# A two-layer graph and expert network on one core: the vector engine's expert chain is interleaved with scores and statistics in the first pass

## What is computed

```
x = x + _L0_gnn_ref(_layernorm(x), adj, W, a)     # attention over neighbours, elu
x = x + _L0_ffn_ref(_layernorm(x), ...)           # 8 experts, top 2 of each row, gelu
x = x + _L1_gnn_ref(_layernorm(x), adj, W, a)     # attention over neighbours, relu
x = x + _L1_ffn_ref(_layernorm(x), ...)           # 32 experts, the best one of each row, relu
```

## Time and profile before

| | us |
|---|---|
| median of three runs | 1150.54 (1149.45 to 1150.75) |
| the profiled execution, its own time | 1146.29 |
| its span from first to last instruction | 1144.6 |

### The profile page before, as it was taken

One profiled execution on the slowest core, in us unless ns is written; L12 is line 12 of the kernel. 1 busy time (PEld: TensorE's weight loads), 2 busy tenths in 40 slices (PEclk: granted clock), 3 DMA queues, 4 the chain that ended last, 5 costly groups with the idle time before them and its releaser, 6 DMA issues. The chain is left out here.

```text
span 1144.6 us, 27026 instructions
## 1 busy us (share of the span) xinstructions
PE 918.4 (80%) x6709; PEld 815.7 (71%) x6709; DVE 790.8 (69%) x3511; ACT 699.9 (61%) x2364; POOL 774.0 (68%) x1039
## 2 busy tenths in 40 slices
PE   5988889887379999999996599999984377656683
PEld 4777778776279999999996488888873255435463
DVE  6689999998569999999996168888887122221122
ACT  3999999896055555555554599999981143323320
POOL 4447887777728777877878017777887366666665
PEclk9999999988589999999999799999995565775655
DMA  9234432213257777878772212233312343232200
GB/s 210 64 98 146 145 102 74 62 53 112 83 162 209 204 205 206 204 201 210 200 202 74 66 38 76 76 80 87 80 40 74 82 121 94 80 87 84 66 21 37
DMA packets 144906, 129.22 MB, mean 113 GB/s; under 512 B 26522, under 2 KB 116511, under 8 KB 144755
## 3 DMA queue, kind: packets, MB, share of 16 engines
q1 hardware_dynamic: 124114, 91.94, 31.9%
q0 software_dynamic: 17760, 34.20, 8.5%
q10 hardware_dynamic: 2880, 1.35, 0.4%
HBM read 82.74 MB, written 47.48 MB: 114 GB/s over the span
## 5 line engine op out<-in xcount | busy, mean ns | idle before, releaser
L546 POOL DMA_INDIRECT xs<-staged,dst x256 | 260.7, 1018 | 76.9 <-issue 68.3
L1258 ACT ACTIVATE hT<-bank,wt 128x128 f32<-128x128 f32 x620 | 177.1, 369 | 123.1 <-PE bank L1488 86.4
L619 POOL DMA_INDIRECT out<-oq,xq x144 | 145.0, 1007 | 96.4 <-DVE oq L1157 57.4
L597 POOL DMA_INDIRECT x2d<-ob,xi x155 | 164.0, 1058 | 42.8 <-issue 28.5
L1470 PE MATMUL bank<-xnT,wt 128*128 128x128 f32 x1240 | 167.5, 279 | 11.1 <-ACT hT L1258 10.0
L1488 PE MATMUL bank<-w2s,hT 128*128 x1240 | 166.3, 277 | 0.6 <-ACT hT L1258 0.5
L1470 PEld LDWEIGHTS bank<-xnT,wt 128*128 128x128 f32 x1240 | 152.9, 194 | 13.9 <-issue 13.3
L1488 PEld LDWEIGHTS bank<-w2s,hT 128*128 128x128 f32 x1240 | 151.5, 193 | 1.5 <-issue 1.1
L1157 DVE SCALAR_TENSOR_TENSOR oq<-bank,xq 128x512 f32<-128x512 f32 x36 | 24.9, 692 | 173.5 <-remote 95.8
L1207 ACT ACTIVATE p<-bank,nm 128x128 f32<-128x128 f32 x256 | 105.0, 411 | 17.6 <-DVE nm L792 14.4
L1305 ACT ACTIVATE xnqT<-bank 128x512 f32<-128x512 f32 x36 | 21.5, 596 | 153.0 <-PE bank L1357 70.8
(11 more groups left out here) (262 smaller groups left out, 2249.5 us busy)
## 6 DMA issues: line engine op xcount, KB each, us to landing
wt<-wpd SPq DMA_DIRECT2D x155, 258.0 KB
xi<-xs SPq DMA_DIRECT2D x155, 66.0 KB
xq<-xs SPq DMA_DIRECT2D x144, 66.0 KB
xb<-x2d SPq DMA_DIRECT2D x32, 258.0 KB
xb<-in_x SPq DMA_DIRECT2D x32, 256.0 KB
wpd<-w1c SPq DMA_DIRECT2D x56, 129.0 KB
xs<-staged,dst POOLq DMA_INDIRECT x256
x2d<-ob,xi POOLq DMA_INDIRECT x155
```

Of the source, the lines that this page charges most:

```text
L546: pool.indirect_dma_start(out=xs[l], out_offset=bass.IndirectOffsetOnAxis(ap=dst[b % ND][:, c:c + 1], axis=0), in_=stag[s][:, q, 0:ROW], i ...
L597: pool.indirect_dma_start(out=x2d, out_offset=bass.IndirectOffsetOnAxis(ap=xi[t % NXI][:, ID:ID + 1].bitcast(U32), axis=0), in_=ob[:, t % ...
L619: pool.indirect_dma_start(out=orow, out_offset=bass.IndirectOffsetOnAxis(ap=xq[j % NXQ][:, q, ID:ID + 1].bitcast(U32), axis=0), in_=oq[j % ...
L1258: last = act.activation(hT[t % 2][:, j, :], HID[t % 2][:, j, :], ACT.Gelu, bias=wt[t % NW][:, c:c + 1])
```

## The change

On DVE, `pair0` is now cut in 13 parts with a semaphore `pair` of its own. In a heavy step `two_experts` puts one other operation between each two parts: `nmax`, `nm`, `qq`, `staged`, the four `bn_stats` of the new rows and the four of input group n+2 (before, the statistics of n+1 stood at the start of the next step). In a light step `nmax`, `nm`, `qq` and `staged` stand ahead of `places`, and `lgb` behind it. On PE the ranks move from the end of the heavy step to the light step, behind its attention product, and `rows_turned` always comes one step later, behind the next scores. On ACT `th` comes behind `ee` and `rl`. At the start POOL zeroes only the column of `vt` that nothing else writes, DVE makes `cmat` before it waits for the weights, and the two layers' weight products use two banks, with a semaphore count each, behind the first turn of `xs_`.

```diff
-            pool.memset(vt[:, :, :], 0.0).then_inc(sem("vt_zero"), 1)
+            pool.memset(vt[:, :, H1:H1 + 1], 0.0).then_inc(sem("vt_zero"), 1)
...
+            def pair0(b, part):
...
+                if part > 0:
+                    dve.wait_ge(r, 12 * b + part)
+                if part == 0:
+                    dve.tensor_tensor(L, ge3(lgb, k, E0), rows(cl[0], k, E0), ALU.add).then_inc(r, 1)
+                elif part == 1:
+                    dve.reduce_max(ma[:, 0:w], L, AX.X).then_inc(r, 1)
...
+            def two_experts(n, b):
+                pair0(b, 0)
+                pair0(b, 1)
+                if n - 1 < NG:
+                    heights(n - 1)
+                pair0(b, 2)
+                if n - 1 < NG:
+                    limits(n - 1)
+                pair0(b, 3)
+                if n - 4 < NG:
+                    bounded(n - 4)
+                pair0(b, 4)
+                if n - 4 < NG:
+                    residual(n - 4)
+                for q in range(G):
+                    pair0(b, 5 + q)
+                    if n - 4 < NG:
+                        after(dve, "x1", n - 4)
+                        stats(1 - first_of_two(n - 4 + APART), stag[(n - 4) % NS], [q])
+                for q in range(G):
+                    pair0(b, 9 + q)
+                    if n + 2 < NG:
+                        dve.wait_ge(sem(f"x_in{(n + 2) % NX}"), 16 * ((n + 2) // NX + 1))
+                        stats(first_of_two(n + 2), xb[(n + 2) % NX], [q])
...
+                    if l == 0 and i not in PART[0][0]:
+                        if 0 < i - 1 < NG:
+                            heights(n - 1)
+                            limits(n - 1)
+                        if 0 <= i - 4 < NG:
+                            bounded(n - 4)
+                            residual(n - 4)
+                        if i in PART[0][3]:
+                            places(PART[0][3][i])
...
-                    if l == 0 and i - 1 in PART[0][2]:
-                        rows_turned(n - 5)
+                    if l == 0:
+                        rows_turned(l, n - 5)
...
+                    if l == 0 and i - 1 in PART[0][2]:
+                        ranks(l, PART[0][2][i - 1])
...
+                    if l == 0 and i == 0:
+                        graph_weights()
```

More of the change, by code:

```diff
@@ L642, in mark, with stats @@
                 return op
-            def stats(half, src):
-                for q in range(G):
+            def stats(half, src, own=range(G)):
+                for q in own:
                     last = dve.bn_stats(st[:, half * G + q, :], src[:, q, 0:P])
@@ L818, in best @@
                 link(dve.reduce_max(key[:, 0:k * G], c, AX.X))
[L820 to L831, removed]
@@ L1313, in _, with graph_weights @@
         def _(pe):
[L1314 to L1319 removed]
+            def graph_weights():
+                for l in range(2):
+                    after(pe, "wraw", l)
+                    pe.matmul((SM, AB[0])[l][:, 0:P + 2], cmat[:, :], wraw[l][:, :], start=True, stop=True).then_inc(sem("wcat_ps"), 1)
+                pe.wait_ge(sem("identb"), 1)
             def routing_weights(part):
@@ L1358, in turn, with ranks, rows_turned @@
                 last.then_inc(sem(done), 1)
+            def ranks(l, b):
+                B, w = NB[l], ORDER[b][1] * G
+                after(pe, "oh", b)
+                o = oh[:, 0:w * B].rearrange("p (g e) -> p g e", e=B)
+                r = SM[:, 0:(w + 1) * B].rearrange("p (g e) -> p g e", e=B)
+                pe.matmul(r[:, 0:w, :], below[:, :], o, start=True, stop=False, skip_group_check=True)
+                for q in range(w):
+                    last = pe.matmul(r[:, q + 1:w + 1, :], onesb[:, :], o[:, q:q + 1, :].broadcast_to([P, w - q, B]),
+                                     start=False, stop=(q == w - 1), skip_group_check=True)
+                last.then_inc(sem("rank_ps"), 1)
+            def rows_turned(l, m):
+                if l * NG <= m < (l + 1) * NG:
+                    after(pe, "x1", m)
+                    after(pe, "pt", min(m + 2, l * NG + NG - 1))
+                    after(pe, "x1T", m - 1)
+                    turn(XP, stag[m % NS], "x1_ps")
             def graph_layer(l):
                 E = (E0, E1)[l]
-                B = NB[l]
-                def rows_turned(m):
-                    if l * NG <= m < (l + 1) * NG:
-                        after(pe, "x1", m)
-                        after(pe, "pt", min(m + 2, l * NG + NG - 1))
-                        after(pe, "x1T", m - 1)
-                        turn(XP, stag[m % NS], "x1_ps")
                 for i in range(NG + 8):
@@ L1435, in graph_layer @@
                         last.then_inc(sem("lg_ps"), 1)
[L1436 to L1449 removed]
+                    if l == 1 and i in PART[1][2]:
+                        ranks(l, PART[1][2][i])
+                    if l == 1:
+                        rows_turned(l, n - 4)
                 w = 8 if l == 0 else 2
```

120 lines of the change are left out of this document (65 added, 55 removed).

## The result

The changed kernel takes 1162.34 us (median of four runs, 1159.86 to 1170.19), the kernel before beside it 1150.12: a ratio of **1.0115**, 95% interval 1.0087 to 1.0144. It is slower by 1.2%, where a gain to 1135.0 us was forecast.

The account below looks back on a forecast made before the run. DVE was taken to set the pace, with the pass ending on POOL. First transfer at 71.1, POOL's work 203.4 and waits 2.7 put the last `ve` at 277.2, 15.5 us sooner: median 1135.0 us, range 1130 to 1142.

Parts of the forecast that it names:

- the heavy step's `nmax` can start 8.9 us after the light step's `pm`: First pass, new loop over PE: from light `pm` through `lgb`, logits and products to the end of the scores, 8.9 us.
- the loop takes 14.5 us a pair: First pass, new loop over PE: 8.86 us from `pm` to `nmax` plus 5.67 to the next `pm`.
- The 0.86 of the sum: First pass: extra time in a slow-clock window, for eight products taking 1.92 us where they otherwise take 0.97.
- the sum had 6.0: First pass: slow TensorE clock adds 7 x 0.86 = 6.0 us to the loop, if all falls in it.
- the loop over PE binds: Rival, chance 0.20: pairs of steps take 15.1 to 15.3 us, gain 5 to 12.5 us, about 1141 us.
- The start, 4.4 us: Kernel start: without the memset beside DVE's cast, the first `wcat` product comes at 10.9 instead of 15.37, 4.4 us gained.
- The heavy step's 1.65 us of DVE, 14.1 a pair: Heavy step: other work between dependent DVE operations saves 1.65 us, so DVE alone needs 14.1 us a pair.
- The rival by which the chain is not shortened: Rival, chance 0.06: interleaving saves DVE nothing, it keeps 15.9 us a pair, only the start gains, 1146.8 us.
- ACT's 14.5 a pair: First pass: ACT alone needs two steps of 7.12 us and some 0.3 for `th`, 14.5 us a pair.
- POOL follows DVE and costs nothing: First pass: POOL's transfers get `dst` later, but in later pairs POOL is over 1.4 us behind DVE, so no cost.
- Ranks and `rows_turned` cost nothing: PE's order: moved ranks and row turns are covered, as ACT needs `x1T` only 4.5 us after `xT`; cover thin.
- The slower rival, 0.05: Rival, chance 0.05: TensorE at 1.2 GHz most of the pass; 1153 us at 16.5 a pair, 1178 at 18.6.

Follow-up runs that it names:

- `lgb_ahead`: Changed kernel with `lgb` first in the light step and PE's ranks waiting for it: 0.984 where the kernel before takes 1092 to 1094 us, 1.0123 where 1146 to 1150.
- `lgb_and_turned_again`: Changed kernel with `lgb` first in the light step and that step's new rows turned at its end: 1.0001 where the kernel before takes 1146 to 1150 us.
- `start_alone`: Kernel before with only the start's edits (narrow memset, `cmat` before the weights' wait, a count per layer's product): 0.9957, then 0.9963.
- `rows_first`: Changed kernel with `lgb` first, the light step's rows turned at its end, and `qq` and `staged` ahead of the heavy `nmax`: 0.9832 where the kernel before takes 1092 to 1094 us.

## Why the prediction was wrong

**The step that failed** is "the heavy step's `nmax` can start 8.9 us after the light step's `pm`", and with it the claim that the loop takes 14.5 us a pair. In the first profile, at a granted clock of 1.00 (the light `pm`, the heavy `nmax` and the next light `pm`):

```profile
173.72 0.28 DVE L762 SCALAR_TENSOR_TENSOR pm<-p 128x128 f32<-128x128 f32 x1
...
185.05 0.69 DVE L791 TENSOR_REDUCE nmax<-bank 128x4 f32<-128x512 f32 x1 [2.19 <-remote]
...
190.72 0.29 DVE L762 SCALAR_TENSOR_TENSOR pm<-p 128x128 f32<-128x128 f32 x1
```

It is 11.33 us from `pm` to `nmax` where 8.9 was worked out, and 5.67 from there to the next `pm`, as forecast. DVE's rows of two pairs on the even chip:

```profile
65.38 0.29 DVE L762 SCALAR_TENSOR_TENSOR pm<-p 128x128 f32<-128x128 f32 x1 [0.16 <-ACT p L1261]
...
74.45 0.68 DVE L791 TENSOR_REDUCE nmax<-bank 128x4 f32<-128x512 f32 x1
...
80.16 0.29 DVE L762 SCALAR_TENSOR_TENSOR pm<-p 128x128 f32<-128x128 f32 x1
...
84.92 0.18 DVE L808 TENSOR_TENSOR lgb<-bank,staged 128x32 f32<-128x32 f32 x1
...
90.88 0.69 DVE L791 TENSOR_REDUCE nmax<-bank 128x4 f32<-128x512 f32 x1 [1.56 <-PE bank L1460]
...
96.62 0.29 DVE L762 SCALAR_TENSOR_TENSOR pm<-p 128x128 f32<-128x128 f32 x1
```

From `pm` to `nmax` it is 9.07 in the first pair and 10.72 in the second, from there to the next `pm` 5.71 and 5.74 (5.67 forecast). `lgb` comes 4.76 after `pm` (4.52 forecast). Two things are missing in my 8.9, one a size and one a mechanism that the prediction did not have:

- *The clock, 1.7 us in such a pair where I had 0.86.* The same kernel's windows of these two pairs, and PE's eight `wa` products in each:

```profile
65.38:80.16 14.78, 13.43 (x106) 11.47 (x105) 13.85 (x75) 14.66 (x50) 10.11 (x12) 1.00 0.40 125
80.16:96.62 16.46, 15.07 (x105) 12.71 (x105) 13.98 (x75) 14.66 (x50) 13.77 (x16) 0.90 0.44 133
```

```profile
72.46 1.05 PE L1459 MATMUL bank<-wa,xT 128*128 128x128 f32 x8
...
87.62 1.92 PE L1459 MATMUL bank<-wa,xT 128*128 128x128 f32 x8
```

  With TensorE at its lower level (1.2 GHz) most products from `wcat` to the scores stretch, not one set of eight. (The 0.86 of the sum is also not what the prediction's own two figures give: 1.92 less 0.97 is 0.95.) Seven of the twelve pairs of this trace have a granted clock of 0.90, so by these rows I put the cost of the clock at some 12 us (7 x 1.7), where the sum had 6.0. On the even chip this and the 0.2 us of `lgb` and the logits leave pairs of 14.8 to 17.3 us, a last `ve` at 287.80 instead of the forecast 277.2, and 0.9971. It was in the list of rivals ("the loop over PE binds", 15.1 to 15.3 a pair), too cheap by 0.6 to 0.8. It is tempting to say that the loop feeds itself: `lgb_ahead`, where PE does not stand for `lgb`, keeps a granted clock of 1.00 from 66.79 to 216.92, and this kernel, where PE pauses 0.56 us ahead of the logits in the second pair shown, falls in more than half of them. But other pairs speak against it. PE idles 3.3 to 3.5 us in each of these two, the first of the changed kernel and the second of `lgb_and_turned_again`, both on late chips, and the granted clock is 1.00:

```profile
173.72:190.72 17.00, 13.54 (x104) 11.46 (x103) 14.08 (x80) 14.67 (x51) 12.10 (x15) 1.00 0.22 65
180.19:196.66 16.47, 13.17 (x104) 11.45 (x103) 13.88 (x77) 14.80 (x50) 11.97 (x15) 1.00 0.22 67
```

  The Trainium skill's page TensorE: Matmul & The Clock Gate (HAM oscillation — how this bites in real kernels) describes a kernel in which PE's waits for data bring the clock down; the rows here go both ways, and what makes the clock fall in this pass stays open.

- *The late signals, 1.8 us for the heavy `nmax` and 0.4 for the light one*, on the chip of the first result. At a granted clock of 1.00 the pair from 173.72 to 190.72 takes 17.00 there, against 14.78 on the even chip, and 15.20 in a later pair there that has early-table parts on DVE as this one has. The pass ends at 317.55 and 314.86 in two profiles, on the even chip at 295.90: some 19 to 22 us, more than the 15.5 us that were forecast as the whole gain. Leaving out the transfers takes 30 us off the pass on the late chip and 10 on the even one, 20 apart. That transfers and late signals belong together is shown by this; that the late signals alone make up the 20 us is not.

By the steps of the prediction:

- *The start, 4.4 us:* right (first product 10.98 against 10.9; 0.9957 and 0.9963 alone). The cast takes 0.43, not 0.3.
- *The heavy step's 1.65 us of DVE, 14.1 a pair:* right in size (13.96 to 14.15 busy). The rival by which the chain is not shortened falls, for operations of 0.2 us: DVE is busy 15.12 us in the pair of steps from 150.06 to 165.94 before, and 13.85 to 14.15 here. The Trainium skill's page VectorE: DVE Perf Modes (The DRAIN you can't avoid) has eight copies with a semaphore after each take as long as with one at the end; this trace does not agree.
- *ACT's 14.5 a pair:* right, reached with `lgb_ahead` (14.52, busy throughout).
- *POOL follows DVE and costs nothing:* wrong in the first profile (35.3 us of waits for `dst`) because the loop made it late, right with `lgb_ahead`.
- *Ranks and `rows_turned` cost nothing, "that cover is thin":* true on an even chip for `rows_turned`, where taking it back loses 7 us; the ranks were not tried by themselves. On a late chip `rows_turned` costs the most: taken back on top of `lgb_ahead` it gives 1.2%.
- *The slower rival, 0.05:* its threshold (16.5 us a pair) was about right, since the kernel is slower with 17 to 19 us a pair and a little faster with 16; but that a slower result stood in the list at all was luck, since its mechanism, the clock, is only a part. The larger part, a signal that comes late beside a transfer, is in none of the prediction's rivals. It was in no row that I had read, since in the pass before `nmax` stood 1.6 to 3.8 us behind the end of the scores in nearly every step and hid it. A sign of it could have been seen elsewhere. These are waits of DVE's `oq`, in the last stage, in the kernel before (late chip, 310 to 1140 us) and in `start_alone` on an even chip (310 to 1080):

```profile
DVE oq L1157 <- remote: 95.8, 13, 8.9
```

```profile
DVE oq L1155 <- DMA out<-oq,xq: 58.3, 15, 5.3
```

  In the first, 95.8 us of waits have no releaser that the view could find, while POOL issues the transfers of that stage; in the second, none. That these are the same thing was not tested.

What stays open: why PE's signals are late beside a transfer of rows on some chips and not on others; whether it is the signal or the product that is late; whether signals of other engines are late too; whether the fourth transfer of a group has a part of its own; what makes the granted clock fall; and `rows_first` on a late chip.

## What to carry to other kernels

A reorder that fills an engine's idle links can close a loop that had slack. Before such a reorder is believed, the new loop is to be added up with all its products at TensorE's lower level, not one set of them. A loop that waits on PE should also be left some room: the old order had 1.6 us and more in nearly every step, by accident, and a signal 1.1 us late costs it nothing (0.9989). A wait that the view calls "remote" on a program of one core is to be explained before operations are moved next to it. And one chip's ratio is not the kernel's: this change is 1.0115 on one and 0.9971 on the other.

## What the runs showed of the hardware

Products of TensorE that ended just behind the start of POOL's fourth transfer were followed together, 1.8 to 2.0 us after that start, on some chips (`nmax` 94.06, 111.71, 131.01, 148.87 against transfers at 92.09, 109.73, 129.05, 146.87 in the first profile), and at once on others (`nmax` 105.70 behind scores at 105.62, with a transfer at 105.60). With a power on four columns in place of the transfers the pass takes 335.6 and 334.8 us on the two, with the transfers 365.6 and 345.0. The kernel before takes 1146 to 1150 us on the ones and 1092 to 1094 on the others, though its first pass ends at about the same time (`filli` at 300.75, and at 295.64 with the 4 to 5 us of the start taken off).

TensorE's granted clock stayed at 1.00 for 150 us in a row in `lgb_ahead`, with PE busy 13.5 of 14.5 us. It was also 1.00 over a pair in which PE was busy 13.54 of 17.00 us, and 0.89 in the kernel before over 16 us with 14.46 busy. What makes it fall is not shown.

VectorE was busy 15.12 us in a pair of steps with its dependent short operations in a row, and 13.85 to 14.15 us with the same operations spread among others.
